# The feed-forward part of a gated cross-attention block, in two fp16 parts for each operand

## The reference

```python
x = x + tanh(g_xattn) * xattn(layernorm(x), ctx, mask, ...)      # 16 heads of 32, 128 keys per batch
x = x + tanh(g_ffn) * ffn(layernorm(x), ...)
# ffn(u), with EPS = 1e-5, H = 512, F = 2048, scales per group of 128 rows:
h  = layernorm(u) * ln_gamma + ln_beta
w1 = (fc1_q - 128) * fc1_scales            # 512 x 2048, integers 0..127
w2 = (fc2_q - 128) * fc2_scales            # 2048 x 512
y  = silu(h @ w1 + fc1_bias)
z  = y @ w2 + fc2_bias
ffn = u + 0.5 * z
```

## Time and profile before

| | us |
|---|---|
| median of 3 runs (1148.72 to 1150.44) | 1150.15 |
| the profiled execution | 1149.18 |
| its span on the core | 1147.4 |
| PE busy in it | 1076.1 (94%) |
| DVE, ACT, POOL busy | 635.3, 388.8, 329.3 |

### The profile page before, as it was taken

How to read it: one execution, slowest core, us unless ns; L and a number is a source line. 1 busy time by engine, 2 the same in 40 slices (tenths; PEclk the granted TensorE clock), 3 DMA queues, 4 the chain that set the end, 5 groups by cost and what they waited for, 6 DMA issues and landing times.

```text
span 1147.4 us, 15101 instructions
## 1 busy us (share of the span) xinstructions
PE 1076.1 (94%) x5179; PEld 843.3 (73%) x5179; DVE 635.3 (55%) x1050; ACT 388.8 (34%) x612; POOL 329.3 (29%) x338
## 2 busy tenths in 40 slices
PE   5687989989899878999999999999999999999998
PEld 3454766667666557888888888888888888888887
DVE  5668878878897757775334335335235235235212
ACT  3466757667676633331121121121111111111110
POOL 4445567567575441202101102102102102012000
PEclk9889999999999998999999999999999999999999
DMA  7665657657665659302002002001100100200100
GB/s 261 160 180 149 184 158 225 178 159 229 179 192 171 192 193 327 145 1 74 1 1 74 1 1 72 3 1 40 36 1 30 45 1 1 74 1 1 38 1 37
DMA packets 61185, 109.31 MB, mean 95 GB/s; under 512 B 9368, under 2 KB 10560, under 8 KB 60608
## 3 DMA queue, kind: packets, MB, share of 16 engines
q1 hardware_dynamic: 58632, 104.11, 29.7%
q10 hardware_dynamic: 2488, 4.34, 1.1%
HBM read 72.51 MB, written 33.55 MB: 92 GB/s over the span
## 4 chain that ended last, share of the span: by engine, by line
PE 61%; DVE 1%; issue 0%; ACT 0%; DVEq 0%
PE ps_z L1306 10%; PE ps_z L1308 10%; PE ps_z L1307 10%; PE ps_y L221 10%; PE ps_y L223 10%; PE ps_y L222 10%; PE ps_h L1320 1%; DVE x_in L1426 0%; DVE x L1389 0%; DVE y_hi L1366 0%; DVE w_lo L178 0%; DVE w_f L172 0%; ACT w_hi L163 0%; DVE y_lo L1368 0%; DVEq L48 0%
## 5 line engine op out<-in xcount | busy, mean ns | idle before, releaser
L1366 DVE CAST y_hi<-y_f 128x512 fp32r<-128x512 f32 x128 | 63.2, 494 | 380.1 <-ACT y_f L1341 380.0
L1341 ACT ACTIVATE y_f<-ps_y,cols 128x512 f32<-128x512 f32 x128 | 88.2, 689 | 540.6 <-PE ps_y L223 540.4
L1306 PE MATMUL ps_z<-w_hi,y_hi 128*128 128x512 f32 x512 | 203.0, 397 | 3.2 <-DVE w_lo L178 3.2
L221 PE MATMUL ps_y<-xt_hi,w_hi 128*128 128x512 f32 x512 | 199.5, 390 | 1.5 <-PEq L258 1.5
L1308 PE MATMUL ps_z<-w_hi,y_lo 128*128 128x512 f32 x512 | 200.4, 391 | 0.0
L1307 PE MATMUL ps_z<-w_lo,y_hi 128*128 128x512 f32 x512 | 200.1, 391 | 0.0
L222 PE MATMUL ps_y<-xt_lo,w_hi 128*128 128x512 f32 x512 | 199.3, 389 | 0.0
L223 PE MATMUL ps_y<-xt_hi,w_lo 128*128 128x512 f32 x512 | 199.3, 389 | 0.0
L1306 PEld LDWEIGHTS ps_z<-w_hi,y_hi 128*128 128x128 f32 x512 | 96.7, 189 | 22.5 <-DVE w_lo L178 3.6
L221 PEld LDWEIGHTS ps_y<-xt_hi,w_hi 128*128 128x128 f32 x512 | 96.3, 188 | 21.8 <-issue 1.9
L1308 PEld LDWEIGHTS ps_z<-w_hi,y_lo 128*128 128x128 f32 x512 | 96.7, 189 | 20.6
(11 more groups left out here) (176 smaller groups left out, 1578.9 us busy)
## 6 DMA issues: line engine op xcount, KB each, us to landing
q_pack<-q_dram SPq DMA_DIRECT2D x96, 256.0 KB, 4.0
q_dram<-q_hi SPq DMA_DIRECT2D x32, 256.0 KB, 3.5
q_dram<-q_lo SPq DMA_DIRECT2D x32, 256.0 KB, 4.2
x_dram<-x_out SPq DMA_DIRECT2D x32, 256.0 KB, 4.8
x_res<-in_x SPq DMA_DIRECT2D x30, 256.0 KB, 4.6
q_raw<-in_L_ffn_fc_q SPq DMA_DIRECT2D x6, 1024.0 KB, 17.9
s_raw<-in_L_ffn_fc_scales SPq DMA_DIRECT2D x6, 1024.0 KB, 17.1
x_in<-in_x SPq DMA_DIRECT2D x4, 1024.0 KB, 7.6
```

Source lines behind the costliest of these rows:

```text
L221: nc.tensor.matmul(out, s_hi, m_hi, start=(k == 0), stop=False)
L1306: nc.tensor.matmul(ps_z[t][:, :], hi, w2_hi[:, f, :], start=(f == 0), stop=False)
L1341: nc.scalar.activation(y_f[f % 2][:, :], ps_y[f % 2][:, :], ACT.Silu, bias=b1_c[:, f:f + 1]).then_inc(y_f_ready, 1)
```

## The change

All four feed-forward operands become fp16 parts of 2 bytes each. fp16 has a narrow range, so each operand is multiplied by a factor that brings it inside it, and the sums are multiplied back: ps_y by `y_unscale` within silu's instruction, ps_z by `z_unscale` where it is added to the residual. The factors are worked out on the chip from the greatest absolute values of gamma and beta, of the two scale tables and of fc1_bias. Since the parts are smaller, the raw integers and scales get two slots each in place of four, and SP now waits until a slot is free ahead of each later load. Four further edits go with it: two loads of the scale tables on ACT's queue, reductions and 13 small instructions on VectorE, two small matmuls in the setup with moved waits, and on GpSimd `row_scales` stands ahead of the low parts of the probabilities.

```diff
-            w1_hi, w1_lo = (fb(n, [P, FB // GROUP, KB, GROUP * P], F32R) for n in ("w1_hi", "w1_lo"))
-            w2_hi, w2_lo = fb("w2_hi", [P, FB, D], F32R), fb("w2_lo", [P, FB, D], F32R)
+            w1_hi, w1_lo = (fb(n, [P, FB // GROUP, KB, GROUP * P], F16) for n in ("w1_hi", "w1_lo"))
...
+            ht_hi.append(sb(f"ht_hi{n}", [P, KB, CHUNK], F16))
...
+        y_hi = [sb(f"y_hi{n}", [P, CHUNK], F16) for n in range(4)]
...
+            nc.scalar.activation(hi, full, ACT.Identity, scale=(w1_scale, w2_scale)[w]).then_inc(w_hi_ready, 1)
...
+            nc.vector.scalar_tensor_tensor(out=lo, in0=full, scalar=(w1_scale, w2_scale)[w], in1=hi,
+                                           op0=ALU.mult, op1=ALU.subtract).then_inc((w1_ready, w2_ready)[w], 1)
...
             def first_maxima():
                 values()
+                pe.wait_ge(row_most_ready, 1)
+                nc.tensor.transpose(ps_s[1][0:4, 0:P], row_most[:, :], ident[:, :]).then_inc(most_turned, 1)
...
             def first_scores():
                 pe.wait_ge(v_bounded, 1)
                 nc.tensor.matmul(ps_s[0][:, 0:1], all_ones[:, 0:P], v_bound[:, :], start=True, stop=True).then_inc(v_summed, 1)
-                pe.wait_ge(v_scaled, 1)
-                pe.wait_ge(k_pack_loaded, 16 * 3 * HG)
-                pe.wait_ge(minus_ones, 1)
+                pe.wait_ge(diagonal_ready, 1)
+                nc.tensor.matmul(ps_s[1][:, 0:4], all_ones[0:4, 0:P], diagonal[:, :], start=True, stop=True).then_inc(most_spread, 1)
...
+            def ffn_numbers():
+                dve.wait_ge(most_ready, 1)
+                link(nc.vector.tensor_scalar(most, most, 1e-30, None, ALU.max))
+                link(nc.vector.reciprocal(inv_most[:, 0:3], most[:, 0:3]))
...
+                nc.vector.tensor_scalar(z_unscale, z_unscale, half_gate[:, :], 1.0 / (W_RANGE * Y_RANGE),
+                                        ALU.mult, ALU.mult).then_inc(scales_ready, 1)
...
+                              0: value_parts, 6: ffn_numbers})
...
+                if k % KB == 3 and (not isinstance(i, int) or 2 * i + k // KB + 3 >= 2):
+                    row_scales(i, k // KB + 3)
                 if real(i, k, UNITS) and not in_tail(i, k):
                     probabilities_lo(i, k, 2)
                     probabilities_lo(i, k, 3)
                 if real(i, k - 1, UNITS):
                     outputs_lo(i, k - 1)
-                if k % KB == 3 and (not isinstance(i, int) or 2 * i + k // KB + 3 >= 2):
-                    row_scales(i, k // KB + 3)
...
+                if isinstance(i, int) and i == 0 and k == -2:
+                    load_w1(sp, 1)
+                    load_w2(sp, 1)
+                    sp.wait_ge(w1_ready, 2)
+                    load_w1(sp, 2)
+                if isinstance(i, int) and i == 0 and k == LOAD + 1:
+                    sp.wait_ge(w2_ready, 2)
+                    load_w2(sp, 2)
+                    sp.wait_ge(w1_ready, 4)
+                    load_w1(sp, 3)
+                if isinstance(i, int) and i == 0 and k == LOAD + 4:
+                    sp.wait_ge(w2_ready, 4)
+                    load_w2(sp, 3)
...
-                nc.vector.tensor_copy(y_hi[f % 4][:, :], y_f[f % 2][:, :]).then_inc(y_hi_ready, 1)
+                nc.vector.tensor_scalar(y_hi[f % 4][:, :], y_f[f % 2][:, :], y_scale, None, ALU.mult).then_inc(y_hi_ready, 1)
...
-                    nc.vector.tensor_tensor(out_t, ps_z[t][:, :], out_t, ALU.add).then_inc(out_ready, 1)
+                    nc.vector.scalar_tensor_tensor(out=out_t, in0=ps_z[t][:, :], scalar=z_unscale, in1=out_t,
+                                                   op0=ALU.mult, op1=ALU.add).then_inc(out_ready, 1)
```

More of the change, by code:

```diff
@@ L100, in build @@
         maxima = [sb(f"maxima{n}", [P, TT, HG], F32) for n in range(2)]
-        xt_hi = [sb(f"xt_hi{n}", [P, KB, CHUNK], F32R) for n in range(2)]
-        xt_lo = [sb(f"xt_lo{n}", [P, KB, CHUNK], F32R) for n in range(2)]
+        ffn_scales = sb("ffn_scales", [P, D], F32)
+        most, w1_scale, w2_scale, y_scale, y_unscale, z_unscale = (
+            ffn_scales[:, at:at + n] for at, n in ((0, 4), (4, 1), (5, 1), (6, 1), (7, 1), (8, 1)))
+        inv_most, y_bound = ffn_scales[:, 9:12], ffn_scales[:, 12:13]
+        h_gain, h_shift = ffn_scales[:, 16:16 + KB], ffn_scales[:, 16 + KB:16 + 2 * KB]
+        with ExitStack() as rows32:
+            xt_hi = [sb(f"xt_hi{n}", [P, KB, CHUNK], F32R, rows32) for n in range(2)]
+            xt_lo = [sb(f"xt_lo{n}", [P, KB, CHUNK], F32R, rows32) for n in range(2)]
+        ht_hi, ht_lo = [], []
+        for n in range(2):
+            ht_hi.append(sb(f"ht_hi{n}", [P, KB, CHUNK], F16))
+            ht_lo.append(sb(f"ht_lo{n}", [P, KB, CHUNK], F16))
+        w_f = [sb(f"w_f{n}", [P, 2 * D], F32) for n in range(2)]
+        y_hi = [sb(f"y_hi{n}", [P, CHUNK], F16) for n in range(4)]
+        y_lo = [sb(f"y_lo{n}", [P, CHUNK], F16) for n in range(4)]
         GROUP = 4
@@ L148, in w_parts @@
             if w == 0:
-                first = 2 * n % GROUP * P
-                parts = [a[:, 2 * n // GROUP, :, first:first + 2 * P] for a in (w1_hi, w1_lo, s1_raw, q1_raw)]
+                group = 2 * n // GROUP
+                cols = slice(2 * n % GROUP * P, (2 * n % GROUP + 2) * P)
+                parts = [w1_hi[:, group, :, cols], w1_lo[:, group, :, cols], s1_raw[group % 2][:, :, cols], q1_raw[group % 2][:, :, cols]]
                 full = w_f[at % 2][:, :].rearrange("p (k c) -> p k c", k=KB)
             else:
-                parts = [a[:, 2 * n:2 * (n + 1), :] for a in (w2_hi, w2_lo, s2_raw, q2_raw)]
+                group, blocks = 2 * n // GROUP, slice(2 * n, 2 * (n + 1))
+                held = slice(2 * n % GROUP, 2 * n % GROUP + 2)
+                parts = [w2_hi[:, blocks, :], w2_lo[:, blocks, :], s2_raw[group % 2][:, held, :], q2_raw[group % 2][:, held, :]]
                 full = w_f[at % 2][:, :].rearrange("p (f d) -> p f d", f=2)
@@ L1245, in step @@
                 c, f = k // FB, k % FB
-                if isinstance(i, int) and i == 0 and k in (-2, LOAD + 1):
-                    half = FB // GROUP // 2
-                    for n in range(half) if k == -2 else range(half, 2 * half):
-                        if n > 0:
-                            load_w1(sp, n)
-                            load_w2(sp, n)
+                if isinstance(i, int) and i == 0 and k == -2:
[11 more added lines that the diff above has]
+                    load_w2(sp, 3)
                 if f == LOAD and real(i, FB * (c + 1)):
```

111 lines of the change are left out of this document (76 added, 35 removed).

## The result

The changed kernel takes 1104.95 us (median of 3 runs, 1101.9 to 1105.33) against 1150.15 us before: the ratio is 0.9602, with an interval from 0.9573 to 0.9631. The prediction was 1107 us. Run again later, beside other runs of the kernel before, the changed kernel gave 1101.71 us and 0.9566 (0.9548 to 0.9584).

> The changed kernel as it is, once more, as the yardstick for the experiments on this chip: 1101 to 1106, ratio 0.960. If it comes out at 1097 or less, the first experiments' distances to it were measured against the wrong number.

A forecast was written before the change was run, and what follows sets the result against it. TensorE was taken as the bound in the feed-forward and nearly in attention. Terms -32.3 - 13.8 + 3 + 0 = -43.1 took the profiled 1149.18 us to 1106.1, median 1107; forecast 1100 to 1114 (chance 0.5), range 1096 to 1127.

The forecast's parts named there:

- The feed-forward matmuls: TensorE in the feed-forward: fp16 matmuls start 0.216 us apart instead of 0.2267, saving 32.3 us over 3020 of them.
- rivals 1, 4 and 5: Feed-forward matmuls: pitch unchanged, 1139 us, chance 0.08; weight loads exposed, about 1240, 0.04; successive matmuls overlapping columns, 860, under 0.01.
- The rest of a step and the raw loads: Feed-forward: other VectorE and ScalarE work stays covered by TensorE and raw loads with fewer slots stay hidden, 0 us.
- The row scales: Attention: earlier scales on GpSimd cut TensorE's stalls by 9.8 us and clock loss by 5.5, p_lo lateness costs 1.5: -13.8.
- the far end: Largest gain allowed for the moved row scales in attention: -9.8 of stall and -11.5 of clock loss, -21.3 us.
- wrong above 1 us: Sign against the forecast: weighted values in attention waiting more than 1 us for GpSimd's p_lo.
- the eight waits: Attention: TensorE's waits for maxima, read as once per chunk, 21.3 us in 8 times in all.
- `ffn_numbers`, +3: Attention step 6: 13 small VectorE instructions ahead of the maxima cost 2.3 us, up to 4.6 with lower clock; +3 taken.
- The setup: Setup: the factors' reductions, transpose and small matmul, with TensorE's moved wait, cost 0 in all, between -2 and +2 us.
- rival 2: Attention: moved row scales bring nothing, since later p_lo delays weighted values or VectorE loses the time elsewhere; 1121 us, chance 0.17.
- rival 3: Clock stays full after shorter attention stalls and fp16 feed-forward matmuls are near their columns; 1098 us, chance 0.17.

The follow-up runs named there:

- experiments 1 and 2: Kernel before with only the GpSimd row scales moved ahead of the low parts: 1127.11 us, ratio 0.9789; changed kernel with them moved back: 1124.93 us, 0.977.
- experiment 1: Kernel before with only the GpSimd row scales moved ahead of the probabilities' low parts, feed-forward still fp32r: 1127.11 us, ratio 0.9789.
- experiment 3: Changed kernel with the 13 `ffn_numbers` instructions in one block just ahead of queries_lo in the same step: 1092.64 us, ratio 0.9494.
- experiment 4: Changed kernel with `ffn_numbers` cut into parts of 4, 3 and 6 instructions ahead of queries_lo of steps 2, 4 and 6: 1094.37 us, ratio 0.9496.
- experiments 9 and 10: Hidden matmuls of 512 columns split into two of 256, each with its own weight load: kernel before 1170.39 us, changed kernel 1104.76 us.
- experiment 9: Kernel before (fp32r) with each hidden matmul of 512 columns split into two of 256, each with its own weight load: 1170.39 us.

## Why the prediction was right

The time, 1107 against 1104.95, came out of one large term that was right, a gain that I had put too small and two costs that I had put too small. That the total is within 0.2% is luck: single terms are off by up to 7.5 us, and the errors partly cancel.

- **The feed-forward matmuls, -32.3.** Right: the part got 34.6 us shorter. The distance is 0.2158 us, predicted 0.216; 3072 x 0.0109 = 33.5 us. A chunk, from one first transpose to the next, takes 84.85 us (724.00 to 808.85), predicted 84.7. The distance puts rivals 1, 4 and 5 out. By the Trainium skill, "TensorE: Matmul & The Clock Gate", section "Back-to-back issue gap", the rule of columns / 2.4 plus 2.5 ns was to give 0.2158 us; for fp16 the trace agrees, and at 256 columns the same rule gives 0.1092, as measured. The section calls this the gap of a matmul by itself and says that it over-counts in a stream of load and matmul pairs; the stream here keeps to it. The fp32r rows disagree with it, at both widths.
- **The rest of a step and the raw loads, 0.** Right. From the first hidden matmul to 760 us TensorE has two waits, for the first part of w2 (3.62 us, before 3.21) and one of 0.2 us; none is for a load. The instructions of a step did get longer, by the pages: silu 777 ns for 689, y_hi 547 for 494, y_lo 806 for 753. TensorE covers them.
- **The row scales, -13.8.** The mechanism was right and the size was not: -21.3 by the timeline, -19 to -25 us by experiments 1 and 2. That the far end that I gave is -21.3 too is chance; it was added up from other parts. The step that failed is "TensorE's stall falls by as much, from 3.3 to 1.1 us". I took VectorE's wait of 2.18 us off a stall of 3.27 and kept the difference. Counted from the unit's own scores on TensorE (192.86 us before, 193.88 after), x_norm starts 1.81 us behind them before and 1.06 ahead of them after, 2.9 us earlier: the wait of 2.18, and about 0.6 us by which TensorE's unit itself comes later behind its new wait for p_lo. x_norm then takes 2.35 us where it took 2.92, and the p_lo pair 1.25 where it took 1.70. So the maxima start 3.9 us earlier (8.55 and 4.65 us behind the scores), more than the stall of 3.27, and it goes completely, and with it the lower clock of which I had counted half. VectorE in the timeline of the kernel before, then of the changed one:

```profile
199.18 1.70 DVE L873 TENSOR_TENSOR p_lo<-p_f,p_hi 128x512 f16<-128x512 f32 x2
...
201.41 1.27 DVE L836 TENSOR_REDUCE maxima<-ps_max 128x4 f32<-128x512 f32 x2
```

```profile
196.76 1.25 DVE L907 TENSOR_TENSOR p_lo<-p_f,p_hi 128x512 f16<-128x512 f32 x2
...
198.53 1.28 DVE L870 TENSOR_REDUCE maxima<-ps_max 128x4 f32<-128x512 f32 x2
```

Why the two are shorter no run shows alone. The new wait for p_lo is 0.5 to 0.8 us per chunk, predicted 0.3; "wrong above 1 us" did not occur. One reading was wrong without harm to the sum: of the eight waits only five, 15.2 us, stand behind row scales; the other three, 0.63, 3.04 and 2.38 us from 333 us on, are of another kind, and the 3.04 and the 2.38 are still there.
- **`ffn_numbers`, +3.** +7.15: 4.05 us of wait and about 3 of lower clock behind it. The count of 13 by 0.1 to 0.2 us was right for ten of them. The failed step is "Linked ones follow each other by 0.20 us, the others by about 0.1: 2.3 us": the rows behind it are of 128x2 instructions of the setup, and at the new place three instructions on 128x4 stand beside GpSimd's low parts and take 3.3 us in all.
- **The setup, 0.** +0.7 at unit 4 in the profile shown, but about +2.4 in the middle of nine profiles, just outside the ±2. The step that failed is "so little is gained: 0 in all": it counted the waits and left out the clock, which is 0.67 to 0.77 behind them where it was 0.87.
- The other cases: rival 2 (nothing from the scales) is ruled out by experiment 1; rival 3 (full clock, 1098) had the right picture of the layer norm's stalls, but the fp16 matmul is not nearer its columns than 0.2158 us, and `ffn_numbers` cost more than its 2 us; with that moved, experiment 3 gave 1092.6.

So the errors in the profile shown, -7.5, +4.2, -2.3 and +0.7 us in this order (scales, numbers, feed-forward, setup) and +0.7 at the end of attention, sum to -4.2: a span of 47.3 us less where the sum said 43.1.

## What to carry to other kernels

A stall that is released by a late engine is not shortened by the lateness alone: lay the whole unit out once more with the earlier start and see whether anything is still last. Put small helper instructions where their engine waits anyway and where GpSimd is not working, and price them from rows with the same neighbours. A change with two parts can owe as much to the small one: time each part by itself before crediting the name that it goes by.

## What the runs showed of the hardware that was not expected

- VectorE instructions on 128x4 fp32 take 0.22 us with GpSimd idle and 0.5 to 1.3 us beside its tensor_tensor, ending within 0.03 us of the end of one of GpSimd's, by either of two operations. So does one on 128x1 with two inputs (0.51 us for 0.16, experiment 4). Those with one input on 128x1 and 128x3 keep their 0.14 to 0.17 us beside the same work.
- If the cost is a fixed part plus the columns, the fixed part of an fp32r matmul with 128x128 weights is 12.5 ns and that of fp16 2.6 ns, by the distances at 512 and 256 columns (experiments 9 and 10).
- A weight load's duration is not the distance that it allows: in experiment 9 the loads are 0.19 us each and start 0.12 us apart, as the matmuls do. "Nearly fills the time of its matmul", as I put it for 188 ns, was no reason. The view is that of the weight loads in the timeline:

```profile
800.32 0.19 PEld L223 LDWEIGHTS ps_y<-xt_hi,w_lo 128*128 128x128 f32 x1
800.44 0.19 PEld L221 LDWEIGHTS ps_y<-xt_hi,w_hi 128*128 128x128 f32 x1
```
